# The opening of a patch-embedding, linear-attention and feed-forward kernel: term rows picked on chip, row 0 first, four scales on ScalarE, first values in two banks

## The reference, cut to what matters

```python
def tok(x, gamma, beta, W, b):           # x (64, 2, 104, 104)
    lu, ru, ld, rd = shifts(x)            # x moved by 4 pixels on both axes, zero padded
    concat = jnp.concatenate((x, lu, ru, ld, rd), axis=1)          # 10 channels
    mean, var = mean_and_var(concat, axis=(1, 2, 3))                # one of each per image
    normed = (concat - mean) * jax.lax.rsqrt(var + 1e-7) * gamma[None] + beta[None]
    y = conv(normed, W, window 8x8, stride 8) + b                   # (64, 128, 13, 13)
    return y.reshape(64, 128, -1).transpose(0, 2, 1)                # 169 tokens an image
h = concatenate([cls_tok for each image, tok(x)], axis=1)           # (64, 170, 128)
n = layernorm(h)
q, k, v = n @ Wq.T, n @ Wk.T, n @ Wv.T
for t in range(170):                      # attention with a running state, S starts as memory0
    S = S + 0.01 * einsum('bd,be->de', v[:, t], k[:, t])            # summed over the images
    h[:, t] += S @ q[:, t]
h = h + ffn(layernorm(h))                 # for this width it gives back its input
```

## Time and profile before

| | us |
|---|---|
| median of 3 runs (229.25 to 229.37) | 229.32 |
| the profiled execution | 229.03 |
| its span, from first to last instruction | 227.2 |

### The profile page before, as it was taken

One profiled execution on the slowest core, in us unless ns is written; L12 is line 12 of the kernel. 1 busy time (PEld: TensorE's weight loads), 2 busy tenths in 40 slices (PEclk: granted clock), 3 DMA queues, 4 the chain that ended last, 5 costly groups with the idle time before them and its releaser, 6 DMA issues.

```text
span 227.2 us, 4909 instructions
## 1 busy us (share of the span) xinstructions
PE 198.8 (87%) x1558; PEld 169.3 (75%) x1558; DVE 154.2 (68%) x760; ACT 112.1 (49%) x244; POOL 157.6 (69%) x124
## 2 busy tenths in 40 slices
PE   0299997899899999999999999999999999988500
PEld 0289886677688899888888888899888888876300
DVE  2658983351576786687777768579649866976971
ACT  6002211345334555565656585575566558475642
POOL 1049869899982899968999579669999235253130
PEclk9999999999999999999999999999999999999955
DMA  6999957913113005162053602012101211201434
GB/s 171 369 426 421 423 239 113 372 75 82 77 17 143 3 0 179 34 191 58 3 165 83 185 23 46 22 28 49 46 3 46 48 27 24 46 4 46 109 79 100
DMA packets 16543, 26.00 MB, mean 114 GB/s; under 512 B 1319, under 2 KB 13277, under 8 KB 16262
## 3 DMA queue, kind: packets, MB, share of 16 engines
q1 hardware_dynamic: 15836, 25.18, 34.7%
q10 hardware_dynamic: 682, 0.51, 0.7%
HBM read 19.77 MB, written 5.92 MB: 113 GB/s over the span
## 4 chain that ended last, share of the span: by engine, by line
PE 64%; DMA 12%; POOL 9%; DVE 8%; issue 2%; ACT 2%; SPq 0%; DVEq 0%; ACTq 0%; POOLq 0%
PE conv L462 29%; DMA rows<-x_windows 12%; PE vr_ps L504 11%; PE first_ps L514 9%; PE outs L531 9%; POOL scaled L382 7%; PE turn L494 4%; DVE scaled L382 2%; PE conv L468 2%; DVE images L819 1%; DVE state L790 1%; DVE state L798 1%; POOL g_low L1091 1%; DVE ln_stats L824 1%; PE conv L504 1%
## 5 line engine op out<-in xcount | busy, mean ns | idle before, releaser
L462 PE MATMUL conv<-scaled,wt 128*128 128x256 f32 (+3 forms) x460 | 116.0, 372 | 9.9 <-DMA wt<-weight 9.9
L382 POOL TENSOR_TENSOR scaled<-rows,gam 128x832 f32<-128x832 f32 x60 | 93.8, 1586 | 6.2 <-PE conv L462 4.2
L462 PEld LDWEIGHTS conv<-scaled,wt 128*128 128x128 f32 x460 | 77.1, 193 | 18.0 <-DMA wt<-weight 9.9
L666 ACT ACTIVATE values<-vr_ps,rstd 128x256 f32<-128x256 f32 x78 | 37.0, 475 | 64.8 <-PE vr_ps L504 54.5
L1101 POOL TENSOR_TENSOR rstd<-var,powers 128x8 f32<-128x8 f32 (+2 forms) x20 | 30.4, 1518 | 23.9 <-DVE var L810 23.9
L790 DVE TENSOR_TENSOR state<-first_ps,state 128x128 f32<-128x128 f32 x80 | 23.3, 291 | 31.5 <-PE first_ps L514 26.8
L674 ACT ACTIVATE images<-images,ln_shift,ln_gain 128x128 f32<-128x128 f32 x82 | 37.9, 484 | 4.8 <-DVE ln_shift L858 4.8
L504 PE MATMUL vr_ps<-w_high,g_low 128*128 128x256 f32 x80 | 32.0, 400 | 0.4 <-ACT values L666 0.4
L1091 POOL TENSOR_TENSOR g_low<-g_t,g_high 128x512 fp32r<-128x512 f32 x21 | 26.8, 1274 | 6.7 <-ACT g_high L653 5.9
L779 DVE BATCH_NORM_STATS2 ln_stats<-images 128x6 f32<-128x128 f32 x85 | 23.7, 284 | 6.7 <-ACT images L660 6.6
L798 DVE TENSOR_TENSOR state<-second_ps,state 128x128 f32<-128x128 f32 x80 | 22.6, 282 | 2.1 <-issue 0.3
(11 more groups left out here) (147 smaller groups left out, 236.6 us busy)
## 6 DMA issues: line engine op xcount, KB each, us to landing
rows<-x_windows SPq DMA_DIRECT2D x13, 864.0 KB, 5.6
out<-images SPq DMA_DIRECT2D x41, 128.0 KB, 2.4
images<-x_rows SPq DMA_DIRECT2D x3, 624.0 KB, 21.8
...
```

The lines of the kernel that those rows point to most:

```text
L382: return eng.tensor_tensor(scaled[:, s, at:at + N], window, gains, ALU.mult)
L462: last = pe.matmul(conv_ps[g % 2][:, at:at + n * B], wt[:, s], scaled[:, s, a % RING:a % RING + n], start=first, stop=(g < EARLY and s == ...
L666: act.activation(values[:, t % VALUE_SLOTS].rearrange("p a e -> p (a e)"), vr_bank(t)[:, 0:2 * E], ACT.Identity, scale=rho_of(t)).then_inc ...
```

## The change

- **Loads.** The first transfers are now: gamma for row 0 alone (32 KB), the left half of row 0 (416 KB, what shift 0 reads), the weights, the right half, the offsets above row 0 for 64 partitions only (224 KB; VectorE fills the rest with zeros), then gamma, beta, the small matrices (384 KB instead of 512), row 1. The images come in seven chunks, three ahead of row 2. Row 4 is issued behind row 3, ahead of the term rows. Owners and bias go by ScalarE's queue.
- **Term rows.** For groups 0 to 4 TensorE picks them from `term_parts` with 20 small fp32r matmuls against 0/1 matrices (`picks`), and ScalarE copies them to `terms`. Only the rest goes through DRAM, and only L518 waits for it.
- **Scales.** ScalarE scales shift 4 of row 3 and shifts 3 and 4 of row 4, these in shares at the steps of `ROW_4_TOKENS`, and shift 4 of row 2: token by token, 64 columns each, gamma as the scale column. It also scales token 39 alone, the first of row 3, so that group 4 needs nothing else of row 3, and GpSimd's scales of row 3 have 12 tokens (768 columns).
- **Order.** TensorE makes the tables before the weights' products, group 1 before `vr` of the class token, and all of group 4 before the loop. The centred weights and `cls_t` are made by ScalarE. GpSimd's power stands after one scale of row 3, not two.
- **Banks.** The `vr` of tiles 1 and 3 goes to `second_ps`, so it waits for the `values` two before.
- `WARM` is used nowhere.

```diff
-STAT_CHUNKS = [(0, 28), (28, 24), (52, 12), (64, 16), (80, 12), (92, 12)]
+STAT_CHUNKS = [(0, 16), (16, 16), (32, 20), (52, 16), (68, 16), (84, 12), (96, 8)]
...
-LATE_ITEMS = [item for g in range(EARLY - 1, GROUPS) for item in conv_items(g) if g >= EARLY or item[1] >= EARLY_SHIFTS]
+LATE_ITEMS = [item for g in range(EARLY, GROUPS) for item in conv_items(g)]
...
-FIRST = (6, 3, 2, 1, 1, 1, 1, 1)
+FIRST = (2, 2, 1, 1, 1, 1, 1, 1)
...
+BY_SCALAR = ((2, 4), (3, 4), (4, 3), (4, 4))
+ROW_4_TOKENS = {-7: (3, 0, 5), -6: (3, 5, 4), -4: (3, 9, 4), -3: (4, 0, 4), -2: (4, 4, 4), -1: (4, 8, 5)}
+EARLY_TOKENS = TOKENS * EARLY
+CORNER = 3 * N
...
+        picks = sb("picks", [EARLY_TOKENS, EARLY, 2, 2, TERM_ROWS], F32R)
...
+            if t in (1, 3):
+                return second_ps
...
+            if a + n - 1 == CORNER:
+                eng.wait_ge(corner_scaled, s + 1)
+                last -= 1
+            if (last, s) in BY_SCALAR:
+                eng.wait_ge(scaled_by_scalar, BY_SCALAR.index((last, s)) + 1)
+            elif last > 0:
+                eng.wait_ge(scaled_rows, pool_scales(last, s))
...
+            sp.dma_start(gam_first[:], first_gamma).then_inc(first_gamma_in, 16)
+            sp.dma_start(rows[:, 0, 0:N], x_windows[:, 0, 0:N]).then_inc(row_in[0], 16)
+            sp.dma_start(wt[:], weight).then_inc(weight_in, 16)
+            sp.dma_start(rows[:, 0, N:2 * N + 1], x_windows[:, 0, N:2 * N + 1]).then_inc(first_right_in, 16)
+            sp.dma_start(rows[B:P, ROW_SLOTS - 1, N:2 * N + 1], first_offsets).then_inc(first_offsets_in, 16)
             sp.dma_start(gam[:], gamma).then_inc(gamma_in, 16)
-            load_row(0)
-            sp.dma_start(rows[:, ROW_SLOTS - 1, N:2 * N + 1], first_offsets).then_inc(first_offsets_in, 16)
-            sp.dma_start(wt[:], weight).then_inc(weight_in, 16)
+            sp.dma_start(bet[:], beta).then_inc(beta_in, 16)
             sp.dma_start(small[:], smalls).then_inc(small_in, 16)
             load_row(1)
-            sp.dma_start(bet[:], beta).then_inc(beta_in, 16)
             load_images(0)
             load_images(1)
+            load_images(2)
             load_row(2)
-            for i in range(2, len(STAT_CHUNKS)):
-                load_images(i)
+            load_images(3)
+            load_images(4)
+            load_images(5)
+            load_images(6)
...
+            load_row(4)
-                at, src = prod * 2 * TOKENS, parked[0:full * TOKENS, :, part].rearrange("(g j) k e -> (j k) g e", j=TOKENS)
-                sp.dma_start(terms[at:at + 2 * TOKENS, 0:full].bitcast(F32), src).then_inc(terms_in, 16)
+                at, src = prod * 2 * TOKENS, parked[EARLY_TOKENS:full * TOKENS, :, part].rearrange("(g j) k e -> (j k) g e", j=TOKENS)
+                sp.dma_start(terms[at:at + 2 * TOKENS, EARLY:full].bitcast(F32), src).then_inc(terms_in, 16)
-            load_row(4)
...
+                        pe.wait_ge(terms_in, 16 * 2 * PRODUCTS)
...
+                pe.wait_ge(vr_ready, tile_no(t) - (2 if t >= TAIL + PER_GROUP or 0 < t < PER_GROUP else 1))
...
+            pe.wait_ge(centered, 3)
+            pe.matmul(out_ps[:, 0:E], wk_c[:], wq_c[:], start=True, stop=True, skip_group_check=True)
+            pe.matmul(out_ps[:, E:2 * E], center[:], small[:, WV], start=True, stop=True,
+                      skip_group_check=True).then_inc(products_done, 1)
+            pe.matmul(first_ps[:, 0:E], wq_c[:], small[:, MEM], start=True, stop=False, skip_group_check=True)
+            conv_shifts(1, 0, SHIFTS)
             pe.wait_ge(cls_t_ready, 1)
             pe.wait_ge(w_vr_ready, 2)
             pe.matmul(vr_ps[:, 0:2 * E], cls_t[:], w_vr[:], start=True, stop=True).then_inc(vr_done, 1)
-            conv_shifts(1, 0, SHIFTS)
+            pe.wait_ge(table_low_ready, 2)
+            pe.wait_ge(picks_ready, 2)
+            for g in range(EARLY):
+                to = turn_ps[0:TERM_ROWS, g * E:g * E + E] if g < PER_GROUP else second_ps[0:TERM_ROWS, 0:E]
+                for kind in range(2):
+                    for part in range(2):
+                        last = pe.matmul(to, picks[:, g, kind, part],
+                                         term_parts[0:EARLY_TOKENS, 0, kind, part], start=(kind == 0 and part == 0),
+                                         stop=(kind == 1 and part == 1), skip_group_check=True)
+            last.then_inc(picked, 1)
+            conv_shifts(2, 0, SHIFTS)
             pe.wait_ge(vr_ready, 1)
...
-            conv_shifts(2, 0, SHIFTS)
-            conv_shifts(3, 0, 3)
+            conv_shifts(3, 0, 4)
             pe.wait_ge(sums_ready, 2)
+            pe.wait_ge(w_low_ready, 1)
             pe.matmul(out_ps[:, 2 * E:2 * E + 2], small[:, SAME], sums[:], start=True,
                       stop=True).then_inc(image_sums_done, 1)
-            conv_shifts(3, 3, SHIFTS)
+            conv_shifts(3, 4, SHIFTS)
+            conv_shifts(EARLY - 1, 0, 2)
             pe.wait_ge(scale_cols_ready, 1)
             pe.matmul(out_ps[:, 0:B], scale_cols[:], small[:, IDENT, 0:B], start=True,
                       stop=True).then_inc(scale_rows_done, 1)
-            conv_shifts(EARLY - 1, 0, EARLY_SHIFTS)
+            conv_shifts(EARLY - 1, 2, 4)
             pe.wait_ge(own_scales_ready, 1)
+            pe.wait_ge(early_rows_ready, 1)
+            early(0)
+            conv_shifts(EARLY - 1, 4, SHIFTS)
             pe.wait_ge(state_ready, 1)
             pe.matmul(out_ps[:, 0:E], cls_t[:], state[:, STATE_SLOTS - 1, 1], start=True,
                       stop=True).then_inc(out_done, 1)
-            pe.wait_ge(terms_in, 16 * 2 * PRODUCTS)
-            pe.wait_ge(table_low_ready, 2)
-            early(0)
             for t in range(START, TAIL):
...
+            def scale_token(t, s):
+                r, j = t // N, t % N
+                window = rows[:, r % ROW_SLOTS, j] if s == 0 else rows[
+                    :, (r if s < 3 else r - 1) % ROW_SLOTS, N + (s - 1) % 2 + j]
+                return act.activation(scaled[:, s, t % RING], window, ACT.Identity, scale=gam[:, s, t:t + 1])
+            def scale_here(r, s):
+                for j in range(1 if r * N == CORNER else 0, N):
+                    last = scale_part(r, s, j)
+                last.then_inc(scaled_by_scalar, 1)
+            def scale_part(r, s, j):
+                act.wait_ge(row_in[r % ROW_SLOTS], 16 * (r // ROW_SLOTS + 1))
+                act.wait_ge(gamma_in, 16)
+                act.wait_ge(conv_step, SHIFTS * last_group_of_row(r - 2) + s + 1)
+                return scale_token(r * N + j, s)
...
+                if t in ROW_4_TOKENS:
+                    s, first, count = ROW_4_TOKENS[t]
+                    for j in range(first, first + count):
+                        last = scale_part(EARLY_ROWS, s, j)
+                    if first + count == N:
+                        last.then_inc(scaled_by_scalar, 1)
...
             group_out(0)
+            for blk, ps in enumerate((turn_ps, second_ps)):
+                count = P if blk == 0 else PATCHES - P
+                act.wait_ge(tables_done, blk + 1)
+                act.copy(term_parts[0:count, blk, :, 0],
+                         ps[0:count, 0:2 * E].rearrange("p (k e) -> p k e", e=E)).then_inc(table_high_ready, 1)
...
             group_out(1)
+            act.wait_ge(vr_done, 1)
+            act.wait_ge(rho_ready, 1)
+            act.activation(values[:, VALUE_SLOTS - 1].rearrange("p a e -> p (a e)"), vr_ps[:, 0:2 * E], ACT.Identity,
+                           scale=cls_rho[:]).then_inc(vr_ready, 1)
+            act.wait_ge(picked, 1)
+            act.copy(terms[0:TERM_ROWS, 0:PER_GROUP], turn_ps[0:TERM_ROWS].rearrange("p (g e) -> p g e", e=E))
+            act.copy(terms[0:TERM_ROWS, PER_GROUP], second_ps[0:TERM_ROWS, 0:E]).then_inc(early_rows_ready, 1)
+            scale_here(2, 4)
+            group_out(2)
             act.wait_ge(cls_state_done, 1)
             act.copy(state[:, STATE_SLOTS - 1, 1], first_ps[:, 0:E]).then_inc(state_ready, 1)
-            group_out(2)
+            act.wait_ge(row_in[CORNER // N], 16)
+            for s in range(SHIFTS):
+                act.wait_ge(conv_step, SHIFTS * last_group_of_row(0) + s + 1)
+                scale_token(CORNER, s).then_inc(corner_scaled, 1)
+            group_out(3)
             act.wait_ge(image_power_ready, 1)
...
-            group_out(3)
+            scale_here(3, 4)
+            group_out(4)
             for t in range(START, TAIL):
...
+            dve.tensor_copy(picks[:].rearrange("p g k a r -> p (g k a) r"), zeros[0:EARLY_TOKENS, 0:TERM_ROWS].unsqueeze(
+                1).to_broadcast([EARLY_TOKENS, 4 * EARLY, TERM_ROWS])).then_inc(picks_ready, 1)
+            dve.memset(rows[0:B, ROW_SLOTS - 1, N:2 * N + 1], 0.0).then_inc(offsets_zero, 1)
...
+            for kind in range(2):
+                for prod, part in enumerate((0, 1, 0)):
+                    at = prod * 2 * TOKENS + kind
```

(11 more changed lines are left out.)

121 lines of the change are left out of this document (71 added, 50 removed).

## The result

The changed kernel takes **227.83 us** (median of 9 runs, 227.04 to 228.78), the kernel before 229.29 in the same job (229.16 to 229.37): a ratio of 0.994, 95% interval 0.9924 to 0.9956. So it is faster by 1.46 us, inside the range, but half of the 3.0 that were forecast. The lowest and the highest of its runs are 1.7 us apart, those of before 0.2. The profiled execution took 227.73, its span is 225.8.

A forecast was written before the change was run, and what follows sets the result against it. TensorE, busy from 60.4 us, was held by the opening and a chain mostly of GpSimd's scales. `early` 2.75 us earlier, h(0) 2.4 and the loop's gain put group 3's turn 3.0 earlier: 226.3 us, range 225.2 to 228.9.

The forecast's parts named there:

- the start: Opening up to the end of group 0's convolution: 13.5 against 16.3, 2.8 us earlier, bounds 1.0 and 3.6.
- with the gap before the second scale I take 13.5: End of group 0's convolution: 12.8 if TensorE never waits, 13.5 with the gap, against 16.3 before.
- about 7.5: Opening: time in us at which row 0's right half, 1,216 KB down the queue, lets VectorE's second scale begin.
- 0.7 to 1.2 earlier: just in time: VectorE's sums of squares, done 0.7 to 1.2 us earlier, ready for TensorE's sums matmul at 33.5 against 34.32.
- Picks: Before the sums matmul: 20 small TensorE matmuls for the term rows cost 1.3 to 2.6 us, taken as 1.6.
- From the sums matmul to `early`: Sums matmul at 33.5, power out at 35.2, first `early` at 38.2 instead of 40.96, without the DMA wait.
- A token on ScalarE: Scaling 64 columns on ScalarE costs 0.24 us, bounds 0.15 and 0.48; thirteen tokens cost 3.1 us.
- From h(0) (42.86) to h(2) (54.29): The loop's first steps: ScalarE becomes the chain, h(0) near 40.8, first `values` at 45.0, h(2) near 52.5.
- Rival A: Second `parked` transfer delays row 3 to near 35.8; `early(0)` gains only 0.5; 228.3 us; chance with half-way cases 0.21.
- Rival B: ScalarE's 26 tokens of row 4 cost 0.48 each in series, 6.2 us more: 232.5 us; chance 0.11.
- Rival C: Several small prices higher (picks 2.2, start 1.6, tokens 0.28) take back 2.8 of 3.0: 229.1 us; chance 0.08.
- a start of 1.6: Third rival's opening: a gain of 1.6 us at the start, 1.2 less than the forecast's 2.8.

The follow-up runs named there:

- the run with fourteen zeros: Changed kernel plus 14 matmuls of zeros on TensorE ahead of group 0's convolution: 227.44 us, 0.9912 of the kernel before.
- the runs with the gap filled: Changed kernel plus zero matmuls between group 0's first and second shift: three alone 227.3 us; nine, with 14 ahead of group 0, 227.44 us.
- three zeros: Changed kernel plus three matmuls of zeros between group 0's first and second shift, none ahead: 227.3 us, 0.9919 of the kernel before.
- the run with the transfer in two parts: Changed kernel with class-token loads moved, zeros ahead (14) and in the gap (9), second parked transfer issued as 32 and 9 rows: 227.1 us, 0.993.
- the run with one bank: Changed kernel with the values of groups 1 and 3 back in the one bank they had before: 227.71 us, 0.9933.
- the runs with both cures: Changed kernel, class-token loads behind the small operand, zeros ahead of group 0 (14) and in its gap (9): 227.52 us; with parked transfer split, 227.1.

## Why the prediction was right in part

**The failed step is the start, in the sentence "with the gap before the second scale I take 13.5".** It was 15.6, and two sizes in it were off. First, the right half: "about 7.5" was 8.93. The sum had counted the bytes in SP's queue down to the right half, at the pace at which 1,286 KB were there at 7.84 before; the class token's small packets, which ran beside them from another queue, took the transfers down to 158 GB/s at 4 us. Without them there it was 7.90. Second, TensorE's slow records. The earlier trace rows showed 11 records in 4.31 us and I moved them to the new start as if they were work to be done once. They are a state of the engine, the lower of its clock's two levels: four records were slow ahead of the stand of 1.2 us that the split row brings, and nine more behind it, from 10.0 to 14.0. In the run with fourteen zeros the granted clock reads 0.50 (1.2 GHz) while the records are 0.43 us apart, and 1.00 (2.4 GHz) at 0.215; the changed kernel's list of changes begins with the rise at 14.04. In all sixteen traces the slow records end at such a rise. Counted from TensorE's first record it came after 2.8 to 6.0 us in the nine traces in which TensorE did not stand before it, and after 5.8 to 9.2 us in the seven with the stand. So with the stand the slow stretch lasts 3 us longer on average, though the two ranges touch.

The Trainium skill (TensorE: Matmul & The Clock Gate, HAM oscillation — how this bites in real kernels) describes such an engine that falls back at waits for DMA and pays for it each time, and advises to arrange the work so that it doesn't wait; the run with fourteen zeros agrees, since its clock fell in a stand of 2.4 us; in the changed kernel the clock did not fall back, the stand only put off its rise. I had looked at the first half of the rule (a slow beginning) and not at what the change does, which is to put a stand into the beginning.

**A second step would have failed behind it: the sums "0.7 to 1.2 earlier: just in time".** They were ready at 34.13; before, TensorE took them at 34.32 after a wait of 0.15. In the changed kernel it was VectorE that was late, by its wait of 1.38 us for `w_high`; that is the late start again. But the images would not have allowed more: the last landed at 31.0 (9.1 + 21.9), where VectorE before had them at 30.95, not 0.8 earlier, and in the runs with the gap filled VectorE waits for them instead (0.82 and 1.52 us with three zeros). 320 KB less stood ahead of them, but over the first 15 us the transfers moved 289 GB/s in place of 310, which is 0.3 MB less. So the queue's saving was spent in the slow start. Moving the class token's loads did not bring it back (291 GB/s), so its cause stays open.

With TensorE's slow stretch cured and nothing else, the time was 227.30 and 227.44, 0.4 to 0.5 us less (the marks of the two traces are 0.4 and 0.0 us earlier, so this much is uncertain); the remaining 1.1 came only when VectorE had less to do.

**What was right**, each by its distance, since all of it stands later by the start's 2.1 us:

- Picks: 1.3 us for 20 (0.066 each, forecast 1.6). Group 0's end to the sums matmul took 20.0 us, forecast 20.0.
- From the sums matmul to `early`: 4.8 us, forecast 4.7, with no wait for the parked rows (before 6.6).
- A token on ScalarE: 13 in 3.21 us, 0.25 each, forecast 0.24; in the loop nine take 2.25. The estimate from rows of 128 columns, taken down by a column operand and 64 columns, was good to 4%.
- From h(0) (42.86) to h(2) (54.29): 11.4 us, forecast 11.7; from there to the mark 4.7, forecast 4.84. ScalarE became the chain as described.
- Rival A did not happen: row 3 was there at 33.1. What its mechanism costs is 0.6 us at most (the run with the transfer in two parts). Rival B is excluded by 0.25 a token. Rival C was of the right form, a slow start, and its "a start of 1.6" is nearest to what happened (0.7), without the dearer picks and tokens.

Where the gain comes from is shown in part by the run without the row 4 shares: without them there is none. The opening was to bring h(0) 2.4 us earlier and brought 0.4; the loop behind it was to add 0.6 and added 1.0. So what is missing of the 3.0 was lost in the opening.

**The spread of 1.7 us** follows the same place, at least in part. In profiled executions with the same list of TensorE instructions up to there, the sixteen records took 5.18, 5.28, 5.62, 5.70, 5.70, 6.52 and 6.58 us. The profiled execution of the run with one bank took 228.61, 0.88 more than the changed kernel's, and its sixteen records 0.88 more. In the kernel before, the slow records lay at the start only and ended at 13.8. But the runs with both cures, whose traces show no slow record of group 0, lie 3.2 and 3.4 us apart, so this is not all of it. What sets where a slow stretch ends was not measured. Nor was it tried whether another order of the image loads would bring VectorE's last chunks earlier.
